# Graph network with two dense adjacency passes on one core: 37 second-layer tiles of the last stretch as three products of rounded halves, squares written over their own adjacency tile

## What is computed

```
h  = relu(layernorm(x))                       # 8192 x 128
h1 = h @ W0 + B0
r  = where((adj < 0.5) & not_eye, adj, 1)
S  = where(mask, exp(-(1/r - 1/mu)^2 / (2 sigma^2)), 0)
x  = x + S @ h1                               # layer 1
h  = relu(layernorm(x))
h2 = h @ W1.T
x  = x + (adj * adj + eye) @ h2               # layer 2
```

## Time and profile before

| | us |
|---|---|
| median of 3 runs (lowest, highest) | 1919.39 (1918.92, 1920.91) |
| the profiled execution, its own time | 1917.86 |
| its span, first to last instruction | 1916.1 |
| PE busy in the span | 1870.4 (98%) |
| VectorE busy | 1688.5 (88%) |
| ScalarE busy | 1656.4 (86%) |

### The profile page before, as it was taken

How to read it: one execution, slowest core, us unless ns; L and a number is a source line. 1 busy time by engine, 2 the same in 40 slices (tenths; PEclk the granted TensorE clock), 3 DMA queues, 4 the chain that set the end, 5 groups by cost and what they waited for, 6 DMA issues and landing times.

```text
span 1916.1 us, 13223 instructions
## 1 busy us (share of the span) xinstructions
PE 1870.4 (98%) x4672; PEld 856.5 (45%) x4672; DVE 1688.5 (88%) x979; ACT 1656.4 (86%) x945; POOL 106.9 (6%) x201
## 2 busy tenths in 40 slices
PE   6999999999999999999999999999999999999998
PEld 4544443444444444444444444444444444444443
DVE  7999999998999999999999999999999857465444
ACT  7999999899999999999999999999999955555321
POOL 0000001000000000000000000000000000000111
PEclk9999999999999999999999999999999999999999
DMA  7568888887888886767767867665665576877895
GB/s 273 192 229 330 299 300 310 321 326 270 309 288 317 293 310 236 291 239 282 267 252 274 298 259 262 226 254 208 235 227 218 203 278 239 312 294 292 294 355 217
DMA packets 84288, 521.16 MB, mean 272 GB/s; under 512 B 11008, under 2 KB 11392, under 8 KB 28032
## 3 DMA queue, kind: packets, MB, share of 16 engines
q1 hardware_dynamic: 68544, 468.94, 66.9%
q0 software_dynamic: 15680, 51.39, 7.1%
HBM read 492.50 MB, written 27.79 MB: 272 GB/s over the span
## 4 chain that ended last, share of the span: by engine, by line
PE 52%; ACT 22%; DVE 18%; issue 6%; DMA 1%; DVEq 0%; POOLq 0%; POOL 0%; SPq 0%
PE p_x L415 20%; PE p_l1b L397 13%; PE p_own L415 9%; PE p_l1a L397 8%; ACT rings L683 7%; ACT rings L688 7%; ACT rings L693 6%; DVE rings L554 6%; DVE rings L547 6%; DVE rings L565 5%; ACT rings L700 1%; PE p_l1a L415 1%; DMA x_buf<-xT 1%; PE p_stat L456 0%; DVE xa_buf L640 0%
## 5 line engine op out<-in xcount | busy, mean ns | idle before, releaser
L554 DVE SCALAR_TENSOR_TENSOR rings<-rings,small 128x2048 f32<-128x2048 f32 x256 | 599.8, 2343 | 21.2 <-ACT rings L688 21.1
L415 PE MATMUL p_x<-rings,h 128*128 128x512 f32 x1344 | 605.4, 598 | 8.8 <-DVE xa_buf L635 4.8
L693 ACT ACTIVATE rings<-rings,small 128x2048 f32<-128x2048 f32 x256 | 533.0, 2082 | 88.1 <-DVE rings L554 87.8
L547 DVE SCALAR_TENSOR_TENSOR rings<-rings 128x2048 f32<-128x2048 f32 x256 | 584.5, 2283 | 0.6
L683 ACT ACTIVATE rings<-rings,small 128x2048 f32<-128x2048 f32 x256 | 509.6, 1991 | 12.8 <-DVE rings L547 8.4
L565 DVE TENSOR_TENSOR rings<-rings 128x2048 f32<-128x2048 f32 x176 | 401.7, 2283 | 104.2 <-PE p_x L415 58.8
L688 ACT ACTIVATE rings<-rings 128x2048 f32<-128x2048 f32 x256 | 487.7, 1905 | 5.0
L397 PE MATMUL p_l1b<-rings,h 128*128 128x512 f32 x1024 | 458.9, 594 | 0.0
L397 PE MATMUL p_l1a<-rings,h 128*128 128x512 f32 x1024 | 458.7, 594 | 0.0
L415 PEld LDWEIGHTS p_x<-rings,h 128*128 128x128 f32 x1344 | 256.7, 192 | 331.4 <-issue 318.5
L397 PEld LDWEIGHTS p_l1b<-rings,h 128*128 128x128 f32 x1024 | 195.0, 191 | 245.3 <-issue 243.2
(11 more groups left out here) (73 smaller groups left out, 333.0 us busy)
## 6 DMA issues: line engine op xcount, KB each, us to landing
rings<-adjT SPq DMA_DIRECT2D x439, 1024.0 KB, 5.6
xa_buf<-acc_dram POOLq DMA_DIRECT2D x77, 256.0 KB, 5.6
acc_dram<-xa_buf POOLq DMA_DIRECT2D x74, 256.0 KB, 5.4
x_buf<-xT SPq DMA_DIRECT2D x32, 256.0 KB, 5.0
outT<-xa_buf POOLq DMA_DIRECT2D x16, 256.0 KB, 5.6
acc_dram<-y_buf POOLq DMA_DIRECT2D x15, 256.0 KB, 4.9
y_buf<-acc_dram POOLq DMA_DIRECT2D x13, 256.0 KB, 5.7
acc_dram<-x_buf POOLq DMA_DIRECT2D x1, 256.0 KB, 5.2
```

Of the source, the lines that this page charges most:

```text
L415: last = pe.matmul(out[:, :], h2[:, it.source * G + g, :], block_of(q_ring, it.m % Q_RING, g), start=(it.first and g == 0), stop=(it.last ...
L547: dve.scalar_tensor_tensor(out=tile(s_ring, t % S_RING), in0=tile(a_ring, slot), scalar=CUTOFF, in1=tile(a_ring, slot), op0=ALU.is_lt, op1 ...
L554: dve.scalar_tensor_tensor(out=v, in0=v, scalar=neg_2c, in1=v, op0=ALU.add, op1=ALU.mult).then_inc(squared, 1)
L693: act.activation(v, v, ACT.Exp, bias=exp_bias, scale=neg_k).then_inc(sens_done, 1)
```

## The change

- `q_ring` is gone. `a_ring` has eight slots instead of five, and a square overwrites its adjacency tile there, in the whole kernel. A load into a slot now waits until TensorE has multiplied the item that held it (`q_used`); if the slot held only a layer 1 tile it waits for `premask` as before. The square of an own item waits until its tile is premasked.
- In the last row of layer 1 the masked tiles use three slots of `s_ring` instead of seven (`DENSE_RING`), `premask` comes in the middle of a step's items instead of at the step's start, `log` behind ScalarE's squares, and own items in the middle of a step.
- From step 240 on ScalarE makes all squares but those of diagonal tiles.
- 37 of these 90 items are "split": 19 in the dense steps, 18 in the tail, about every second item whose source is 10 or more. For each, `halves` (on VectorE, in the place behind the next item) copies the square into a tile of type float32r, a float32 rounded to fewer bits (the high half, one of three tiles that lie where four of the slots of `s_ring` came free), and subtracts that from the square into a low half over the adjacency slot. `split_h2` does the same once for each of the sources 10 to 15 of `h2`. TensorE then makes three float32r products for each 128 source nodes: high with high, high with low, low with high. The product of the two low halves is left out. That is twelve products for a split item, where there were four float32 products (eight records).
- A final chain is added to its running sum three items after its last one, not one.

```diff
-A_RING = 5
+A_RING = 8
 S_RING = 7
-Q_RING = 3
+DENSE_RING = 3
+DENSE_SLOT = LAST % S_RING
+SPLIT_STEP = {10: 3, 11: 3, 13: 5, 12: 7, 14: 12, 15: 16}
+SPLITS = [it for it in ITEMS if it.step >= LAST + SPLIT_STEP.get(it.source, STEPS) and it.row != it.source
+          and it.m % 5 % 2 == 0]
     if it.step >= S_STEPS - NC:
-        it.by = "act" if it.m % 2 else "dve"
+        it.by = "act"
-    ch.evac = max(ch.last_m + (1 if ch.final else EVAC), CHAINS[ch.index - 1].evac if ch.index else 0)
+    ch.evac = max(ch.last_m + EVAC, CHAINS[ch.index - 1].evac if ch.index else 0)
...
                     s, it = LOADS[n - A_RING]
-                    if s is not None:
+                    if it is not None:
+                        sp.wait_ge(q_used, it.m + 1)
+                    else:
                         sp.wait_ge(premasked, s + 1)
-                    if it is not None:
-                        sp.wait_ge(q_by[it.by], it.squares)
...
+            def l2_split(it):
+                out = p_own[it.row % 2] if it.own else p_chain[it.chain.bank]
+                pe.wait_ge(h_split, SPLIT_ORDER.index(it.source) + 1)
+                pe.wait_ge(low_ready, it.split + 1)
+                for g in range(G):
...
+                    pe.matmul(out[:, :], h_high, high, start=(it.first and g == 0), stop=False)
+                    pe.matmul(out[:, :], h_high, low, start=False, stop=False)
+                    last = pe.matmul(out[:, :], h_low, high, start=False, stop=(it.last and g == G - 1))
...
-                if t >= S_RING:
+                if t >= LAST + DENSE_RING:
+                    dve.wait_ge(s_used, t - DENSE_RING + 1)
+                elif t >= S_RING:
                     dve.wait_ge(s_used, t - S_RING + 1)
...
+            def halves(it):
+                squares = tile(a_ring, it.load % A_RING)
+                high = high_ring[it.split % 3]
+                dve.wait_ge(q_by[it.by], it.squares)
+                if it.split < 3:
+                    dve.wait_ge(s_used, LAST)
+                else:
+                    dve.wait_ge(q_used, SPLITS[it.split - 3].m + 1)
+                dve.tensor_copy(high[:, :], squares).then_inc(high_ready, 1)
+                dve.wait_ge(high_ready, it.split + 1)
+                dve.tensor_tensor(low_ring[it.load % A_RING][:, :], squares, high[:, :].bitcast(F32),
+                                  ALU.subtract).then_inc(low_ready, 1)
...
                 for it in AT_STEP[s]:
+                    if dense and it is AT_STEP[s][len(AT_STEP[s]) // 2]:
+                        premask(s)
                     if it.by == "dve":
                         square_adj(it)
+                    if it.m and ITEMS[it.m - 1].split is not None:
+                        halves(ITEMS[it.m - 1])
```

107 lines of the change are left out of this document (87 added, 20 removed).

## The result

The changed kernel takes 1905.91 us (median of four runs, 1901.95 to 1907.57); the kernel before, beside it, 1919.16 (1918.30 to 1920.91). The ratio is 0.9926, with a 95% interval from 0.9914 to 0.9938. So it is faster, by 13.3 us, half of the 26 that the forecast of 1893 us gave it, and outside the range of 1886 to 1904. The profiled execution took 1907.14 us, its span 1905.3.

A forecast was written before the change was run, and what follows sets the result against it. The prediction took TensorE's work to bound the changed stretch: 1917.86 us - 31.2 for split tiles + 4 for tail waits + 1 at item 229 = 1891.7, plus 1.53 to the median, so 1893 us, range 1886 to 1904.

The forecast's parts named there:

- What bounds the kernel: In the changed stretch TensorE's work alone sets the end; each us taken from it is a us of the time.
- What a split tile costs: TensorE: twelve one-pass products cost 2.58 to 2.61 us instead of 3.435; 37 tiles gain 31.2 us.
- the rival of a product as slow as a record: TensorE's split tiles: twelve products take 5.15 us, 37 tiles lose 63 us, 1983 us in all; chance 0.09.
- Dense steps: nothing added: Dense steps: VectorE's 187 us and ScalarE's 197 fit within TensorE's 231, so no time is added.
- the lead covers it: Dense steps 11 to 15: VectorE needs 75 us where TensorE needs 70, yet its lead was to absorb this.
- against: 44 us of room: Dense steps: the argument against queue order costing time, VectorE having 187 us of work in 231.
- rival C: Dense steps: the order of VectorE's and ScalarE's queues costs up to 10 us, 1896 to 1906; 0.18 shared with the loads' rival.
- The tail, 5 us allowed: From item 225 on: 4 us for TensorE's waits and VectorE's lag, from 0 to 9, plus 1 us at item 229.
- the halves of items 252 and 254 behind the squares of 253 and 255: End of the tail: 10 us are left for a load's landing, so TensorE waits between 0 and 5 us.
- rival A: Tail: loads stay at 381 GB/s, items 230 to 255 near the old pace, 1895 to 1905 us; 0.18 shared with the queue-order rival.
- The first 1500 us: Before 1500 us the eight-slot ring was to cost 0, from -2 to +5 us.
- rival D: First 1500 us: the ring of eight starves TensorE, 1% being 15 us, 1906 to 1920; 0.04 with more of the queue-order rival.

The follow-up runs named there:

- e4b: Changed kernel with each float32r product of 512 columns made as two of 256: 1908.27 us, ratio 0.9947 to the kernel before.
- e10: Changed kernel with ScalarE's first square ahead of the sensitivity pass in the last 16 dense steps: 1901.11 us, ratio 0.9908 to the kernel before.
- e11: Changed kernel with VectorE's masking pass one item earlier in dense steps with an even number of items: 1902.47 us, ratio 0.9909 to the kernel before.
- e14: Changed kernel with ScalarE's first square ahead of the sensitivity pass and VectorE's mask one item earlier in even dense steps: 1900.98 us, ratio 0.9903.
- e12: Changed kernel with five running-sum buffers, not four, and the tail's diagonal squares behind the halves of the item before: 1904.66 us, ratio 0.9917.
- e6: Changed kernel with the squares of row 15's ten own tiles in the dense steps made by VectorE, not ScalarE: 1908.64 us, ratio 0.9947.
- e3: Changed kernel with five buffers for the running sums of chains instead of four: 1904.79 us, ratio 0.9927 to the kernel before.
- e15: Changed kernel with both dense-step reorderings (square first, mask early), five running-sum buffers and late diagonal squares in the tail: 1897.85 us, ratio 0.9892.
- e9: Changed kernel with the 19 splits of the dense steps alone, the tail's 18 plain float32 again: 1911.84 us, ratio 0.9959.
- e1: Kernel before with the ring of eight and squares in place alone, nothing split, old order: 1921.46 us, ratio 1.0011.
- e2: Changed kernel with no item split, all products of tiles plain float32: 1920.79 us, ratio 1.0011 to the kernel before.

## Why the prediction was wrong

**What bounds the kernel: right.** TensorE set the end; what it was given and what it had to wait is found again in the distances, to some 0.5 us.

**What a split tile costs: the mechanism right, the term mis-sized.** One pass suffices, and the rival of a product as slow as a record (1983 us) is out. But the pace was 0.227 us, not 0.2147 to 0.217. The step that failed is "if a float32r product is one pass, it costs between half a record and 0.217 us": the 0.005 us that the earlier trace rows leave as the fixed part belong to a record of two passes, and a float32r product has about 0.011 of its own (e4b). 12 products x 37 tiles x 0.012 us is 5.3 us of gain that was never there.

**"Dense steps: nothing added": wrong, by 4.9 us.** The sums were not the fault: the low half took the 2.29 us assumed, the high one only 1.22 for 2.28, and between the two centrings, 214 us apart, ScalarE worked 155 us and VectorE 150, where 197 and 187 of 231 had been reckoned. By totals there was more room than forecast. The step that failed is the inference from room in the total to none lost: "the lead covers it", and "against: 44 us of room". Both engines work in order, and each step holds two hand-overs from VectorE to ScalarE and back. Their lead is cut short by each other (shown by e10, e11 and e14), and by the rows of waits also by the chain additions, which hold VectorE for TensorE (36 us in the dense steps of the changed kernel), and by the ring of three (7.7 us); what these two cost was not tested. That was rival C, which had the right mechanism and a price of up to 10 us, but was kept out of the forecast by a sum. e14 gives 3.9 of the 4.9 back by order alone.

**The tail, 5 us allowed, 6.3 lost: size nearly right, cause wrong in part.** Foreseen and found: the halves of items 252 and 254 behind the squares of 253 and 255, in the changed kernel's profile as a wait for VectorE's order (1.8 us, e12), in e6 and e14 also for a load, as forecast; and 1 us at item 229 (0.7 measured). Not foreseen: the buffers of the running sums (2.4 us, e3). The forecast followed the loads of the adjacency and the slots of their ring, but not GpSimd's queue, although the diff moves the addition of a final chain from one item to three behind its last product. That the two errors nearly met the 5 us allowed is luck.

**The loads: right that they don't set the tail's pace.** The changed kernel's DMA engines moved 377 GB/s from 1800 to 1870 us at a share of 0.99, and e15's 397, where the earlier trace rows had 357 and 381, and rival A's tail near the old pace didn't come (e9). In the changed kernel's profile loads issued from 1852.7 to 1870.5 us took longer than before, and ScalarE waits for them, but TensorE doesn't:

```profile
DMA to landing us min/median/max: 8.9/10.4/11.3
```

That is at the lower end of the 10 to 16 us foreseen, for the 8.2 of the earlier trace rows. Where they took 14 us (e14), TensorE did pay for a load.

**The first 1500 us: nearly right, the rest open.** 0 was forecast. TensorE idles for 36.8 us before 1500 us in the changed kernel's profile and for 36.2 in that of before, and row 14 comes 0.5 us later than in the profile of before that starts late too. So rival D at its price of 15 us is out (e1, e2). But the kernels with the ring of eight mostly start late, the profile of before on which the sum stood had the early start, and the medians of e1 and e2 are 2.5 and 1.8 us above that of before. Whether the ring brings this is open.

**Sum.** Forecast gain 26.2 us. Less 5.3 for the pace, 4.9 for the dense steps, 1.3 for the tail beyond what was allowed, and 0.5 before row 14, that is 14.2; the medians show 13.3, and the late start can be the difference. With the right pace, no waits but those that e15 still has, the same sum gives 1919.2 - 25.9 + 0.9 + 2.1 = 1896.3, and e15 measured 1897.85.

## What to carry to other kernels

Before a change takes work from the engine that sets the end and gives it to two others, walk through a few steps of their queues in order, each wait with its releaser, and ask for the longest path around the loop: here it, and not the sum of their work, decided whether TensorE waited. Where TensorE waits after such a change, try another order of the same passes before moving work. A longer wait can cost more than itself: behind one of 3.8 us TensorE worked a whole tile at its lower clock (e6). And a delay added to a buffer's last use has to be followed to whoever loads that buffer next, on whichever queue it stands.

## What the runs showed of the hardware

- A float32r product of 128 x 128 by 512 columns takes 0.227 us and one of 256 columns 0.119 (e4b), where a float32 record of 512 takes 0.4294. Three such products for one of float32 save 20% of a tile (2.73 for 3.43 us), not the 25% of three passes in place of four.
- VectorE writes the high half (a copy of 2048 float32 elements a partition to float32r) at twice the pace of its two-input passes. From the groups by line of the changed kernel (busy us, mean ns, idle before):

```profile
L652 DVE CAST high<-rings 128x2048 fp32r<-128x2048 f32 x37 | 45.2, 1221 | 12.6 <-ACT rings L810 12.5
L654 DVE TENSOR_TENSOR low<-rings,high 128x2048 fp32r<-128x2048 f32 x37 | 84.8, 2292 | 1.3
```

  The Trainium skill, VectorE: DVE Perf Modes, section The perf-mode tier table, has 1227 ns for a float32 copy of 2048 elements within SBUF, and the measurement, with a float32r output, agrees. The forecast had taken 2.28 us from the COPY of 512 elements out of PSUM, the wrong neighbour.
- The core's DMA engines moved more than the 381 GB/s of before when they were asked for more: 397 GB/s over 70 us in e15. The Trainium skill (Perfetto Trace Analysis, section Engine Utilization), of which the prediction weighed only the 358 GB/s, says in its subsection Roofline that this is a core's share when both cores of a pair draw on the memory, and that a core alone is bounded by its DMA engines, at about 435 GB/s. The run agrees with that reading, and the prediction had read the page too shortly.
- TensorE's granted clock fell to 0.50 behind a wait of 3.83 us (e6, for the 5.3 us of one tile) and to 0.51 behind one of 2.45 us (e14, from 1879.7 to 1882.7 us); behind the 2.44 us of the changed kernel it stayed at 1.00. At the lower level a float32r product took 0.43 us.
- A stage in which TensorE never waits repeats to 0.1 us from execution to execution (222.4 and 109.2 in four profiles of three kernels), and so do the dense steps of the changed kernel (214.0 to 214.1 in five profiles). A tail that hangs on when stores and loads land doesn't: it took 100.1 to 103.0 us in five kernels that have the tail of the changed one. The start of the program comes in two forms, some 1.5 to 3.5 us apart.
